# GroupNorm and two-head attention: every row written out, scores of two rows in succession, moments over 24 rows

## The reference

```python
# x: (16, 64, 256, 128) float32; 16 images of 64 rows, 256 tokens a row, 128 channels
def _gn(v, G=32, eps=1e-5):      # mean and variance over an image's rows, tokens and a group's 4 channels
    ...
    return ((g - m) / jnp.sqrt(s + eps)).reshape(v.shape)

def _L0_conv_ref(x, W_qkv, b_qkv):        # H = 2 heads of c = 64 channels
    scale = C ** 0.5
    qkv = jnp.einsum('bglc,dc->bgld', x, W_qkv) + b_qkv
    ...
    score = jnp.einsum('bghlc,bghmc->bghlm', q, k) / scale
    score = jax.nn.softmax(score, axis=-1)
    out = jnp.einsum('bghlm,bghmc->bghlc', score, v)
    ...

x = x + _L0_conv_ref(_gn(x), L0_conv_W_qkv, L0_conv_b_qkv)
```

## Time and profile before

| what | us |
|---|---|
| median of 3 runs | 3922.17 (3921.97 to 3930.68) |
| the profiled execution | 3927.83 |
| its span, first to last instruction | 3926.0 |
| PE busy in it | 3816.5 |
| DVE busy | 3766.5 |
| ACT busy | 3062.5 |
| POOL busy | 2453.1 |

### The profile page before, as it was taken

The page is one execution under the profiler, slowest core; times in us unless marked ns, Lnnn a source line. Parts: engine busy times, 40 slices in busy tenths (PEclk is TensorE's granted clock), DMA queues, the critical chain, the costliest instruction groups (busy, mean ns, idle before and its releaser), DMA issues.

```text
span 3926.0 us, 146106 instructions
## 1 busy us (share of the span) xinstructions
PE 3816.5 (97%) x44133; PEld 2959.7 (75%) x44133; DVE 3766.5 (96%) x7138; ACT 3062.5 (78%) x8193; POOL 2453.1 (62%) x3089
## 2 busy tenths in 40 slices
PE   3999999999999999999999999999999999999999
PEld 2777777777777777777777777777777777777777
DVE  6999999999999999999999999999999999999998
ACT  3777878787787887878778787787877878787786
POOL 1657566575665656666565665656657566576787
PEclk9999999999999999999999999999999999999999
DMA  8999999999999999999999999999999999998989
GB/s 196 209 204 216 211 205 214 204 216 211 207 212 207 212 213 209 211 207 215 211 205 212 206 215 205 210 212 206 213 206 213 212 207 213 205 207 177 176 180 177
DMA packets 2441871, 809.20 MB, mean 206 GB/s; under 512 B 2179072, under 2 KB 2441600, under 8 KB 2441600
## 3 DMA queue, kind: packets, MB, share of 16 engines
q1 hardware_dynamic: 2311040, 679.97, 89.4%
q10 hardware_dynamic: 130560, 125.86, 11.1%
HBM read 134.42 MB, written 134.22 MB: 68 GB/s over the span
## 4 chain that ended last, share of the span: by engine, by line
PE 46%; DVE 34%; issue 13%; DVEq 2%; DMA 1%; ACT 1%; POOL 0%; SPq 0%; ACTq 0%; POOLq 0%
PE s_bank L297 13%; PE qk_bank L275 13%; DVE p_lo L434 13%; DVE neg_max L427 10%; PE o_bank L313 9%; PE v_bank L285 6%; DVE bn L458 4%; PE xt_bank L267 3%; PE v_bank L282 1%; DVE rsum L446 1%; DVEq L458 1%; DVE v_lo L440 1%; DVE o_norm L453 1%; DMA pt_lo<-p_lo 1%; ACT prob L392 1%
## 5 line engine op out<-in xcount | busy, mean ns | idle before, releaser
L598 POOL TENSOR_SCALAR p_hi<-prob 128x1024 f16<-128x1024 f32 x1024 | 1107.6, 1082 | 1419.8 <-ACT prob L392 1061.8
L392 ACT ACTIVATE prob<-s_bank,neg_max 128x256 f32<-128x256 f32 x4096 | 1609.2, 485 | 217.1 <-POOL y_ring L614 95.9
L434 DVE SCALAR_TENSOR_TENSOR p_lo<-prob,p_hi 128x1024 f16<-128x1024 f32 x1024 | 1324.9, 1294 | 50.2 <-POOL p_hi L598 33.4
L427 DVE TENSOR_REDUCE neg_max<-s_bank 128x2 f32<-128x512 f32 x2048 | 1305.5, 677 | 13.0 <-PE s_bank L297 12.3
L373 ACT ACTIVATE qk<-qk_bank,b_in 128x256 f32<-128x256 f32 x2048 | 858.4, 470 | 571.5 <-PE qk_bank L275 566.0
L297 PE MATMUL s_bank<-qk 64*128 64x256 f32 x8192 | 1163.4, 402 | 1.4 <-ACT qk L373 1.1
L275 PE MATMUL qk_bank<-xc,w_norm 128*128 128x256 f32 x4096 | 1159.3, 405 | 0.0
L614 POOL TENSOR_TENSOR y_ring<-image,o_norm 128x256 f32<-128x256 f32 x1024 | 1028.6, 1005 | 4.4 <-DMA out_dram<-y_ring 3.0
L275 PEld LDWEIGHTS qk_bank<-xc,w_norm 128*128 128x128 f32 x4096 | 694.7, 189 | 392.6 <-issue 331.7
L313 PE MATMUL o_bank<-v_hi,pt_lo 128*128 128x65 f16 x8192 | 850.8, 193 | 42.6 <-issue 19.7
L297 PEld LDWEIGHTS s_bank<-qk 64*128 64x128 f32 x8192 | 706.4, 186 | 219.9 <-issue 171.9
(11 more groups left out here) (72 smaller groups left out, 2104.9 us busy)
## 6 DMA issues: line engine op xcount, KB each, us to landing
out_dram<-y_ring SPq DMA_DIRECT2D x512, 256.0 KB, 2.8
image<-in_x_dram ACTq DMA_DIRECT2D x480, 256.0 KB, 3.5
pt_hi<-p_hi SPq DMA_TRANSPOSE x1024, 3.8
pt_lo<-p_lo SPq DMA_TRANSPOSE x1024, 3.3
image<-in_x_dram SPq DMA_DIRECT2D x4, 2048.0 KB, 16.3
w_in<-in_L_conv_W_qkv_dram SPq DMA_DIRECT2D x1, 192.0 KB, 2.5
b_in<-in_L_conv_b_qkv_dram SPq DMA_DIRECT2D x3, 0.5 KB, 2.1
```

The source lines that it names most:

```text
L392: ins = act.activation(prob[:, m, c:c + TOK], s_bank[m][h][:, a * TOK:(a + 1) * TOK], ACT.Exp, bias=neg_max[:, m, h, a:a + 1])
L427: dve.tensor_reduce(neg_max[:, m, h, :], s_bank[m][h][:, :].rearrange("p (a k) -> p a k", a=J), AX.X, ALU.max, negate=True).then_inc(max_d ...
L434: dve.scalar_tensor_tensor(out=p_lo[:, v % 2, :], in0=prob[:, v % 2, :], scalar=P_SCALE, in1=p_hi[:, v % 2, :], op0=ALU.mult, op1=ALU.subt ...
L598: pool.tensor_scalar(p_hi[:, v % 2, :], prob[:, v % 2, :], P_SCALE, 1.0, ALU.mult, ALU.mult).then_inc(phi_done, 1)
```

## The change

- `schedule` has no loops: all 1024 rows, and 8 steps before and after, are written out with constant addresses.
- PE transposes straight from `image`; `x_ring`, POOL's `refill` and its semaphore go.
- PE's step: in an even step scores(i) and scores(i+1), in an odd step none; then qk(i+2), v(i), values(i-3), transpose(i+4).
- ACT: the exponents are of row i rather than i-1, xc of i+3, qk copies of i+2; xc stands ahead of the exponents in even steps, behind them in odd ones.
- DVE: in odd steps neg_max stands first, in even ones behind o_norm; p_lo is of row i-1 rather than i-2 and stands last.
- SP: both transposes and the store are one row further on.
- FINISH is 24, X_AHEAD 3. So the rows 8 to 40 measure, 40 to 64 finish, and LAG falls to 8. Of the 23 operations mostly one stands in a row.

```diff
-    FINISH = 12
+    FINISH = 24
-    X_AHEAD = 2
+    X_AHEAD = 3
...
-        STAT_MM_AT = (0, 2, 6)
-        STAT_OPS_AT = {0: ((1,),), 1: ((2,), (3,), (4,), (5,)), 2: ((6,), (7,)), 3: ((8, 9), (10,), (11,), (12,)),
...
+        STAT_MM_AT = (0, 6, 20)
+        STAT_OPS_AT = {0: ((1,),), 1: ((2,),), 2: ((3,),), 3: ((4,),), 4: ((5,),), 5: ((6,), (7,)), 7: ((8, 9),),
...
+                       14: ((16,),), 15: ((17,),), 16: ((18,),), 17: ((19,),), 18: ((20,),), 19: ((21,),),
+                       21: ((22,), (23,))}
...
+                if bring is not None:
+                    if 0 <= i < 2 * UNROLL:
+                        for c in range(i, CHUNKS - LAG // LOAD_ROWS, 2 * UNROLL):
+                            bring(i, 1, 1, c * LOAD_ROWS)
+                    if coming is not None and row % LOAD_ROWS == 0:
+                        bring(i, *coming)
+                order(run, next_image, i % 2)
+
+            for i in range(-2 * UNROLL, BLOCKS + 2 * UNROLL):
+                step(i)
...
-            def order(run, next_image):
-                run(-2, transpose_low)
-                run(-7, store)
-                run(-1, transpose_high)
+            def order(run, next_image, odd):
+                run(-1, transpose_low)
+                run(-6, store)
+                run(0, transpose_high)
...
-                pe.wait_ge(ring_in, base + (v + 1))
...
-                    mm = pe.transpose(xt_bank[:, j * P:(j + 1) * P], x_ring[:, m, j * C:(j + 1) * C], ident[:, :])
+                    mm = pe.transpose(xt_bank[:, j * P:(j + 1) * P], image[:, par, row, j * C:(j + 1) * C], ident[:, :])
...
-            def order(run, next_image):
-                run(0, scores)
-                run(+1, project_qk)
+            def order(run, next_image, odd):
+                if not odd:
+                    run(0, scores)
+                    run(+1, scores)
+                run(+2, project_qk)
                 run(0, project_v)
                 next_image(0)
                 run(-3, values)
-                run(+3, x_transpose)
+                run(+4, x_transpose)
...
-                run(-1, exponent, 0)
-                run(-1, exponent, 1)
-                run(+2, x_copy)
-                run(+1, qk_copy)
+                if not odd:
+                    run(+3, x_copy)
+                run(0, exponent, 0)
+                run(0, exponent, 1)
+                if odd:
+                    run(+3, x_copy)
+                run(+2, qk_copy)
                 run(0, v_high)
...
-            def order(run, next_image):
-                run(-2, p_low)
+            def order(run, next_image, odd):
+                if odd:
+                    run(0, row_max, 0)
+                    run(0, row_max, 1)
                 run(-4, sums)
                 next_image(0)
                 run(-1, v_low)
                 next_image(1)
                 run(-4, divide)
                 next_image(2)
-                run(0, row_max, 0)
-                run(0, row_max, 1)
+                if not odd:
+                    run(0, row_max, 0)
+                    run(0, row_max, 1)
+                run(-1, p_low)
                 next_image(3)
                 next_image(MEASURE)
...
-            def order(run, next_image):
+            def order(run, next_image, odd):
                 run(0, p_high)
-                run(+6, refill)
                 run(-4, finish)
```

More of the change, by code:

```diff
@@ L159, in schedule, with step @@
         def schedule(eng, order, share=None, bring=None):
-            def step(base, first_row, u, par, row=None, what=None, coming=None):
-                def run(lead, stage, *head):
[L167 to L174, removed]
+            def step(i):
+                img, row = divmod(i, ROWS)
+                par = img % 2
+                what = coming = None
+                if 0 <= img < IMAGES - 1 and STATS_FROM <= row < STATS_FROM + GROUPS:
+                    what = (MEASURE, img + 1, row - STATS_FROM)
+                elif 0 <= img < IMAGES - 1 and row >= ROWS - FINISH:
+                    what = ("finish", img + 1, row - (ROWS - FINISH))
+                if 0 <= img < IMAGES - 1 and row < LAG:
+                    coming = (img + 1, 1 - par, ROWS - LAG + row)
+                elif 0 <= img < IMAGES - 2 and row >= LAG:
+                    coming = (img + 2, par, row - LAG)
+                def run(lead, stage, *head):
+                    v = i + lead
+                    if 0 <= v <= LAST:
+                        stage(*head, 0, v, (v // ROWS % 2, v % ROWS))
@@ L176, in next_image @@
                 def next_image(place):
                     if what is not None and (place == MEASURE) == (what[0] == MEASURE):
[L178 to L205, removed]
-                        step(t * UNROLL + g + STATS_FROM, t * UNROLL + STATS_FROM, u, par, None,
-                             None if last else (MEASURE, img + 1, t * UNROLL + u),
-                             None if final else (img + 2, par, t * UNROLL + (STATS_FROM - LAG + u)))
-                for i in range(FINISH):
-                    row = ROWS - FINISH + i
-                    step(g + row // UNROLL * UNROLL, 0, row % UNROLL, par, row,
-                         None if last else ("finish", img + 1, i), None if final else (img + 2, par, row - LAG))
-                if last:
-                    for i in range(2 * UNROLL):
-                        step(g + ROWS + i // UNROLL * UNROLL, 0, i % UNROLL, par, ROWS + i)
@@ L217, in schedule @@
-            run_image(0, 0, True, False)
-            for img in range(1, IMAGES):
-                run_image(img, img % 2, False, img == IMAGES - 1)
+                        share(0, i, par, what, place)
+                if bring is not None:
[4 more added lines that the diff above has]
+                        bring(i, *coming)
@@ L562, in share @@
                 if what[0] == MEASURE:
-                    if u == 0:
+                    if what[2] == 0:
                         dve.wait_ge(loaded[1 - par], (what[1] - 1 + par) * (8 * CHUNKS)
@@ L599, in p_high @@
                                    ALU.mult).then_inc(phi_done, 1)
-            def refill(base, v, at):
-                par, row = at
-                if not known_below(base, 4 - v):
-                    wait_apart(pool, xt_done, base + (v - 3))
-                pool.tensor_copy(x_ring[:, v % 4, :],
-                                 image[:, par, bass.ds(row, 1), :].rearrange("p a c -> p (a c)")).then_inc(ring_in, 1)
             def finish(base, v, at):
@@ L626, in _, with order @@
             pool.memset(half_ones[:, :], 2.0 / P).then_inc(const_done, 1)
-            pool.wait_ge(first_in[0], 16)
-            def order(run, next_image):
+            def order(run, next_image, odd):
                 run(0, p_high)
-                run(+6, refill)
                 run(-4, finish)
```

13 lines of the change are left out of this document (5 added, 8 removed).

## The result

The changed kernel took 3934.35 us (median of 16 runs, 3929.66 to 3943.81), the kernel before 3926.52 in the same comparison (16 runs, 3919.05 to 3931.35): ratio 1.0021, 95% interval 1.0014 to 1.0029. That is within 0.3% of no change, by the interval a little slower; the forecast was 3845, 2.3% lower. The profiled execution of after has a span of 3928.1 us.

What follows compares the result with a forecast made beforehand. PE bounds plain rows, DVE measuring and finish rows. An image takes 27.8 + 119.7 + 88.4 = 235.9 against 240.8 us: 69 less over fourteen, 11 in the last, 80 off 3927.8 is 3848; said 3845, range 3815 to 3875 (0.50).

Steps and rivals of the forecast that it cites:

- the two holes: On PE: unexplained waits at the first weight loads of scores and of qk, 0.205 us too much each.
- the step of 0.18 a row: On PE: scores of two rows in succession bring a plain row from 3.66 to 3.48 us.
- Loops (a) and (b): Per pair, PE-DVE wait cycles: (a) via v_lo 6.87 us plain, 7.48 measuring; (b) via exponents 6.86 and 7.47.
- Rival 2: Loops (a) or (b) 0.2 us longer than summed: 3920, no change, chance 0.06; half of it 3885, chance 0.12.
- rival 4: PE's drain belongs to each block's first load, whatever stood before: plain rows stay at 3.66, 3940 us; chance 0.04.
- Rival 3: POOL's y_ring meets DVE's p_lo between the two neg_max, 0.45 us more a pair: 4038 us; chance 0.08.
- Transfers: DMA: 225 GB/s needed at 3.48 us a row, 268 seen in a busy stretch; small gain, not counted.
- The moments over 24 rows: Finish stage: 83.5 for PE, 3.3 operations, 0.5 matmuls, 1.1 ACT's wait; 88.4 us, bounds 85 and 91.
- ACT's wait for w_norm: In finish row 21 ACT waits 2.0 us for DVE's w_norm, can lose 0.9 unseen; 1.1 counted.
- x from the image: POOL loses 1024 copies and PE a wait for them, neither on the chain: nothing gained.
- Written out: All rows: code fetched for every row, not once a loop; zero, at most 53 us from above.
- The first image: Row 8, needing all of image 1, comes at 99 us; the image ends at 307 for 305.5: no gain.

Runs made afterwards that it cites:

- no_loads: The changed kernel without the loads of images 2 to 15, transposes and stores kept: 3885.0 us, ratio 0.9894 to before.
- deep_both: The changed kernel with four buffers instead of two for p_hi and for p_lo, each with its own landing semaphore: 3899.6 us, ratio 0.9936 to before.

## Why the prediction was wrong, step by step

- **What bounds the kernel, the two holes, the step of 0.18 a row: right.** 0.38 a pair was measured for 0.36. The rule on draining (the Trainium skill, "TensorEngine Tiling (Array Packing)", section Key Properties) agrees with both halves.
- **Loops (a) and (b), DVE's sums: right in the measuring rows.** Plain pairs come down to PE's 6.92, for 6.96, so neither loop is longer, and measuring pairs take 7.49 for 7.48; rows 8 to 40 come to 119.4 without late landings, for 119.7. Rival 2 (3920) and rival 4 (3940) named times near the result, but by mechanisms that aren't there: longer loops, and a drain that stays in every block. Rival 3's meeting at p_lo did not occur: it takes 1.22 in the measuring pair.
- **Transfers: wrong, 3.1 us an image, 43 us.** The step took 268 GB/s of a 10 us stretch in the first image as what the chip could move, set 225 against it, and counted nothing. That stretch is not the steady mix, and a rate says nothing of when a single transpose lands. Its "some 6 us to land" went by the order of the instructions; POOL needs its buffer back two rows on, and the longest landings (7.09 us in the chain above) reach beyond that: POOL waits up to 7.7. The 43 us are what no_loads gives; four buffers gave back 30 of them. Four buffers don't end it: with loads, rows 8 to 40 without bn take not 3.46 but 3.66 (117.3 / 32), before's plain pace. So even without the moments little of the 0.18 should be left, which no run tests whole.
- **The moments over 24 rows: mis-sized, 2.8 us an image, 39 us.** Operations in even rows were "nothing", since DVE waits for the scores there. But DVE itself is the bound as soon as both rows of a pair carry an operation that meets POOL: without them its sum is 6.40 (7.70 less 0.56 and 0.74, the steps from st to v_lo), with them 7.70, and PE's 6.92 is passed; at the 0.08 of the step behind the st that met nobody (1249.46 to v_lo at 1249.54) it would be 6.56. The prediction compared each edit with a loop and never added DVE's own pair for this stage. The stage takes 91.2 without late transposes, for 88.4; its upper bound was 91. ACT's wait for w_norm was foreseen at 2.0 us, 1.1 of it as cost; it is 17.6 / 15 = 1.2 long, and no run gives its cost apart.
- **x from the image: wrong.** Its "so nothing" looked at the chain alone; it was worth 25 us in the old order, most of it through fewer meetings of POOL's copies with DVE. In the new order nearly every operation meets p_hi or y_ring anyway (45 of those 48).
- **Written out: right, zero** (1.0008).
- **The first image and the end.** The first bn of image 1 stands at 104.3, where near 99 was the sign to look for; the image ends at 309.4 for 307, and the kernel's last steps, behind the last row's qk, take 21.4 for 18.8 before, which was not priced. The last image gained 13 for 11. What makes the first image 4 us longer is not settled: it is 0.7 longer than before's in deep_both and 6.5 in no_loads, whose loads of images 0 and 1 are the same. Executions differ by some us here, so part of it may be chance.

The sum: 3.1 + 2.8 - 0.3 (measuring rows better than forecast) = 5.6, where an image missed by 5.5. It has to close, since the first term is after less no_loads and the others are no_loads less the forecast; what the other runs show is which mechanism each term is. Fourteen are 77 us; with 4 in the first image, 3 at the end and 2 gained in the last, 82, which is what lies between the sum (3848) and the time of the profiled execution (3929.9).

**Where did the expected gain go?** In 32 measuring rows it was never to be had (DVE). In the 24 finish rows DVE took most of it, by meeting POOL. In the 8 plain rows 1.1 us of a possible 1.7 was gained (29.6 before, 28.5 after, 27.9 without loads), and in the last 24 rows 1.0 (92.9 and 91.9). Only the last image kept it, 13 us, against 9 lost by the fourteen before it and 7 at both ends.

## What to carry to other kernels

A shorter step on the bounding engine is worth what the next bound leaves of it, in each stage. So add up, for each stage and for the new period, every engine's own instructions, those in its idle places too, and the bytes that the new pace asks of the transfers, against a rate seen for a whole stage of the same mix. Give a buffer that a DMA reads the time of the longest landing, not of the median. Operations on DVE that meet POOL are priced by where POOL stands in the new order: put them where POOL waits, and look at what a removed POOL copy frees.

## What the runs showed of the chip

- A DVE operation on 128x32 float32: 0.15 us alone, 0.63 to 0.81 beside POOL's p_hi or y_ring. A chain holds over two engines: p_lo stretches p_hi from 1.04 to 2.09 us, and p_hi then holds st.
- With 214 to 220 GB/s of loads, transposes and stores over a stage of 32 rows, transposes landed late enough to hold the rows; with 210 (half the loads' bytes) hardly, with 193 (none) not at all. It is no general limit: 232 stood in 100 us of the first image.
- A median landing of 4.4 us stands beside single ones of over 7, and a buffer's reuse goes by the longest.
- Instructions written out in full, with 5.0 MB more of them moved, cost nothing that could be measured (ratio 1.0008, 0.9997 to 1.0018).
- Scores on halves of the array's rows and blocks on all of it: each change between them costs PE 0.19 us (1.93 for twice 1.06, 0.87 for 1.06).
